# An accumulating DMA takes over half of GpSimd's adds, and ScalarE works thirteen banks ahead instead of seven

## The reference, cut to what matters

```python
e = stack([tbl_f[ids[:, f]] for f in range(39)], axis=1)      # 512 x 39 x 16
prev = e
for k in range(3):
    z = einsum('bmd,bhd->bdmh', e, prev).reshape(b, D, m * h)
    t = einsum('bdc,co->bdo', z, w[k]) + bias[k]
    t = transpose(t, (0, 2, 1)) / sqrt(sum(t * t))             # one norm for each example
    logit.append(t); prev = t
z = sum(concatenate(logit, axis=1), axis=-1)                   # 512 x 384
y = relu(relu([z, dense] @ W1 + b1) @ W2 + b2) @ W3
```

## Time and profile before

| | |
|---|---|
| median of 3 runs | 1070.53 us (1068.94 to 1072.45) |
| profiled execution | 1069.49 us, its span 1067.8 us |
| PE matmul / weight load busy | 97% / 74% of the span |
| DVE / ACT / POOL busy | 91% / 75% / 81% |
| granted TensorE clock | 0.998 of full speed |
| from job 12 to job 116 | 62.4 us for an iteration, eight jobs, nearly the same each time |

### The profile page before, as it was taken

The page is one execution under the profiler, slowest core; times in us unless marked ns, Lnnn a source line. Parts: engine busy times, 40 slices in busy tenths (PEclk is TensorE's granted clock), DMA queues, the critical chain, the costliest instruction groups (busy, mean ns, idle before and its releaser), DMA issues.

```text
span 1067.8 us, 18078 instructions
## 1 busy us (share of the span) xinstructions
PE 1036.7 (97%) x4384; PEld 788.9 (74%) x4384; DVE 971.2 (91%) x3328; ACT 796.2 (75%) x2671; POOL 864.0 (81%) x729
## 2 busy tenths in 40 slices
PE   2999999999999999999999999999999999999998
PEld 0466777878777787877778787777778777788883
DVE  2589999999999999999999999999999999999993
ACT  3476877868778787877778787787878778788872
POOL 6777888988888898888889898888988888576770
PEclk9999999999999999999999999999999999999999
DMA  6630030301403030120303012030300203000000
GB/s 189 158 95 12 3 83 3 84 2 17 126 4 83 3 84 2 22 65 3 83 3 84 1 21 66 3 83 3 84 2 11 75 3 83 1 1 1 1 1 1
DMA packets 59381, 44.02 MB, mean 41 GB/s; under 512 B 39177, under 2 KB 42121, under 8 KB 59146
## 3 DMA queue, kind: packets, MB, share of 16 engines
q1 hardware_dynamic: 51975, 36.49, 13.8%
q10 hardware_dynamic: 2179, 5.07, 1.4%
q0 software_dynamic: 5120, 1.29, 1.3%
HBM read 40.89 MB, written 1.94 MB: 40 GB/s over the span
## 4 chain that ended last, share of the span: by engine, by line
PE 67%; POOL 18%; DVE 6%; issue 5%; ACT 3%; DMA 1%; SPq 0%; POOLq 0%; DVEq 0%; ACTq 0%
POOL sums L415 13%; PE bank_a L705 10%; PE bank_d L705 9%; PE bank_d L707 9%; PE bank_d L706 9%; PE bank_a L707 9%; PE bank_a L706 9%; PE acc L775 8%; POOL gathered L398 4%; DVE sums L939 3%; ACT scaled L539 1%; ACT sums L539 1%; PE turned L748 1%; DVE prev L1004 1%; PE bank_d L876 1%
## 5 line engine op out<-in xcount | busy, mean ns | idle before, releaser
L415 POOL TENSOR_TENSOR sums<-sums,scaled 128x512 f32<-128x512 f32 (+1 forms) x512 | 646.5, 1264 | 140.4 <-ACT scaled L539 103.3
L939 DVE SCALAR_TENSOR_TENSOR sums<-bank_d,x_col,sums 128x128 f32<-128x128 f32 x2304 | 653.4, 337 | 47.1 <-PE bank_d L707 37.0
L539 ACT ACTIVATE scaled<-bank_a,x_col 128x128 f32<-128x128 f32 x1920 | 549.0, 383 | 129.5 <-PE bank_a L707 124.1
L705 PE MATMUL bank_d<-w_hi,prev_lo 128*128 128x512 f32 x640 | 283.9, 444 | 1.5 <-DVE sums L958 1.2
L705 PE MATMUL bank_a<-w_hi,prev_lo 128*128 128x512 f32 (+1 forms) x640 | 268.4, 419 | 3.5 <-ACT scaled L539 0.9
L707 PE MATMUL bank_d<-w_hi,prev_hi 128*128 128x512 f32 x640 | 252.5, 395 | 0.0
L706 PE MATMUL bank_d<-w_lo,prev_hi 128*128 128x512 f32 x640 | 252.2, 394 | 0.0
L707 PE MATMUL bank_a<-w_hi,prev_hi 128*128 128x512 f32 (+1 forms) x640 | 245.3, 383 | 0.0
L706 PE MATMUL bank_a<-w_lo,prev_hi 128*128 128x512 f32 (+1 forms) x640 | 244.9, 383 | 0.0
L539 ACT ACTIVATE sums<-bank_a,x_col 128x128 f32<-128x128 f32 x512 | 146.2, 371 | 75.3 <-PE bank_a L707 75.3
L398 POOL DMA_INDIRECT gathered<-in_table,idx x160 | 174.3, 1089 | 28.5 <-issue 17.9
(11 more groups left out here) (87 smaller groups left out, 537.2 us busy)
## 6 DMA issues: line engine op xcount, KB each, us to landing
x_pairs<-x_scratch SPq DMA_DIRECT2D x135, 156.0 KB
x_pairs<-x_scratch SPq DMA_DIRECT2D x96, 78.0 KB
gathered<-in_table,idx POOLq DMA_INDIRECT x160
x_pairs<-x_scratch SPq DMA_DIRECT2D x92, 22.0 KB
x_scratch<-gathered SPq DMA_DIRECT2D x16, 72.0 KB, 2.2
w_raw<-in_w ACTq DMA_DIRECT2D x1, 1024.0 KB, 5.0
w_raw<-in_w ACTq DMA_DIRECT2D x1, 896.0 KB, 10.1
w_raw<-in_w SPq DMA_DIRECT2D x1, 832.0 KB, 6.8
```

What stands on the lines that cost most here:

```text
L415: nc.gpsimd.tensor_tensor(out=sums[:, n % SUMS, 0:w, :], in0=sums[:, n % SUMS, 0:w, :], in1=scaled[:, a - 1, 0:w, :], op=ALU.add).then_inc ...
L539: op = nc.scalar.activation(to[:, i, :], bank_a[at % A_RING][:, i * UNITS:(i + 1) * UNITS], ACT.Copy, scale=x_of(c, q, a * PER_BANK + i))
L705: nc.tensor.matmul(to, lo, w_h, start=True, stop=False)
L939: nc.vector.scalar_tensor_tensor(out=taken(n, u) if u in LEFT else total, in0=taken(n, u), scalar=x_of(c, q, A_FIELDS + u), in1=total, op0 ...
```

## The change

In jobs 11 to 116 (`is_far`) GpSimd no longer adds four banks. Behind bank 4 it issues one DMA from `scaled` to `scaled` with an add on the way, which adds banks 3 and 4 to banks 1 and 2 (7 fields, 3584 bytes in each of 128 partitions, 448 KB), and then adds banks 1 and 2 to `sums`. These two adds stand five and six A banks behind bank 4 in GpSimd's list: first comes the DMA of the next job, then bank 1 of this job, then bank 2. `scaled` has two sets of buffers for it, for even and odd jobs; the second lies where raw weights lay. ScalarE writes banks 1 and 2 when the adds of the job two before are done, banks 3 and 4 when the DMA of that job is.

The lead grows from 7 to 13 banks over jobs 5 to 10 (six A banks in each of these jobs), and shrinks again over jobs 117 to 122 (four in each). With 13 the three-field bank is made in slot 1, bank 1 in slot 3, bank 2 in slot 4.

The gathers move from behind slots 1 and 2 to behind slots 3 and 4. `high` and `low` move: for layer 1 from behind slot 0 of step 5 to behind slot 3 of step 4, which is where `finish` of layer 1 stands; for layer 2 from behind slot 1 of step 6 to behind slot 0 of step 7. The norm of layer 0 moves on PE from behind place 1 of step 4 to behind place 9 of step 3, and on VectorE its sums and reciprocal come a few fields earlier.

```diff
-LEAD = 7
+LEAD, FAR_LEAD = 7, 13
...
+FAR_FROM, FAR_TO = 11, NJ - 12
+LEADS = [min(max(LEAD, LEAD + n - 5), FAR_LEAD, max(LEAD, FAR_LEAD + FAR_TO - n)) for n in range(NJ + 1)]
+FAR_ADDS = {1: A_BANKS, 2: A_BANKS + 1}
...
+ADDS_BEHIND = {at: [] for at in range(A_BANKS * NJ)}
+for _n in range(NJ):
+    for _a in range(1, A_BANKS):
+        if not is_far(_n):
+            ADDS_BEHIND[A_BANKS * _n + _a].append((_n, _a))
+        elif _a in FAR_ADDS:
+            ADDS_BEHIND[A_BANKS * _n + A_BANKS - 1 + FAR_ADDS[_a]].append((_n, _a))
...
-        FINISHES.append((0, _it + 1, (step_at(_it, 3), 0), (step_at(_it, 3), 14)))
+        FINISHES.append((0, _it + 1, (step_at(_it, 3), 0), (step_at(_it, 3), 8)))
...
-        NORMS.append(([(0, _it + 1)], (step_at(_it, 4), 1), (step_at(_it, 4), 0), (step_at(_it, 4), 6)))
+        NORMS.append(([(0, _it + 1)], (step_at(_it, 3), 9), (step_at(_it, 4), 0), (step_at(_it, 4), 4)))
...
-                HALVES_AT[_k + 1, _c] = (step_at(_c - 1, 5), 0) if _k == 0 else \
-                    (step_at(_c, 6), 1) if _c < CHUNKS - 1 else (step_at(_c, 5), 3)
+                HALVES_AT[_k + 1, _c] = (step_at(_c - 1, 4), 3) if _k == 0 else \
+                    (step_at(_c, 7), 0) if _c < CHUNKS - 1 else (step_at(_c, 5), 3)
...
-            def add_bank(at):
+            def add_banks(at):
+
+                if at >= A_BANKS * NJ:
+                    return
                 n, a = divmod(at, A_BANKS)
-                if n >= NJ or a == 0:
-                    return
-                pool.wait_ge(a_scaled, at + 1)
-                if a > 1:
-                    pool.wait_ge(a_added, ADDS * n + a - 1)
-                w = a_fields_of(a)
-                nc.gpsimd.tensor_tensor(out=sums[:, n % SUMS, 0:w, :], in0=sums[:, n % SUMS, 0:w, :],
-                                        in1=scaled[:, a - 1, 0:w, :], op=ALU.add).then_inc(a_added, 1)
+                if is_far(n) and a == A_BANKS - 1:
+                    pool.wait_ge(a_scaled, at + 1)
+                    nc.gpsimd.dma_start(pair_of(n, 1), pair_of(n, 3), accum_op=ALU.add).then_inc(pair_added[n % 2], 16)
+                for n, a in ADDS_BEHIND[at]:
+                    if is_far(n):
+                        pool.wait_ge(pair_added[n % 2], pairs_added_by(n))
+                    else:
+                        pool.wait_ge(a_scaled, at + 1)
+                    if a > 1:
+                        pool.wait_ge(a_added, ADDED[n, a - 1])
+                    w = PER_BANK if is_far(n) else a_fields_of(a)
+                    nc.gpsimd.tensor_tensor(out=sums[:, n % SUMS, 0:w, :], in0=sums[:, n % SUMS, 0:w, :],
+                                            in1=scaled_of(n, a)[:, 0:w, :], op=ALU.add).then_inc(a_added, 1)
...
+                begin = 1 if n < FAR_FROM else 3
+                for a in range(max(a_count(n), A_BANKS)):
+                    if a < a_count(n):
+                        add_banks(a_first(n) + a)
+                    if begin <= a < begin + per_step and first + a - begin < GATHERS:
+                        gather(it + 2, first + a - begin)
...
-                    if n >= 1:
-                        act.wait_ge(a_added, ADDS * (n - 1) + a)
-                    to = scaled[:, a - 1, :, :]
+
+                    was = n - 1 if n < FAR_FROM else n - 2
+                    if n == FAR_FROM:
+
+                        act.wait_ge(w_lo_made[1], len(W_PIECES[1]))
+                        act.wait_ge(w_lo_made[2], len(W_PIECES[2]))
+                    elif is_far(was) and a > max(FAR_ADDS):
+                        act.wait_ge(pair_added[was % 2], pairs_added_by(was))
+                    elif was >= 0:
+                        act.wait_ge(a_added, ADDED[was, a] if (was, a) in ADDED else added_all(was))
+                    to = scaled_of(n, a)
```

More of the change, by code:

```diff
@@ L67, with is_far, a_first, a_count @@
 JOB_AT = {j: n for n, j in enumerate(JOBS)}
+FAR_FROM, FAR_TO = 11, NJ - 12
+LEADS = [min(max(LEAD, LEAD + n - 5), FAR_LEAD, max(LEAD, FAR_LEAD + FAR_TO - n)) for n in range(NJ + 1)]
+FAR_ADDS = {1: A_BANKS, 2: A_BANKS + 1}
+def is_far(n):
+    return FAR_FROM <= n <= FAR_TO
+def a_first(n):
+    return A_BANKS * n + LEADS[n]
+def a_count(n):
+    return a_first(n + 1) - a_first(n) if n + 1 < NJ else A_BANKS
+ADDS_BEHIND = {at: [] for at in range(A_BANKS * NJ)}
[5 more added lines that the diff above has]
+            ADDS_BEHIND[A_BANKS * _n + A_BANKS - 1 + FAR_ADDS[_a]].append((_n, _a))
+ADDED = {}
+for _at in range(A_BANKS * NJ):
+    for _add in ADDS_BEHIND[_at]:
+        ADDED[_add] = len(ADDED) + 1
+def added_all(n):
+    return ADDED[n, max(FAR_ADDS) if is_far(n) else A_BANKS - 1]
 def step_at(it, q):
@@ L196, in cin_kernel @@
         identity = sb("identity", [128, 128])
-        w_raw = {k: sb(f"w{k}_raw", [128, FIELDS, UNITS]) for k in (1, 2)}
+        used = 28
+        with ExitStack() as first_life:
+            w_raw = {k: first_life.enter_context(nc.sbuf_tensor(f"w{k}_raw", [128, FIELDS, UNITS], f32)) for k in (1, 2)}
+        scaled_odd = []
+        for k in (1, 2):
+            sb(f"raw_rows{k}", [128, used, UNITS])
+            scaled_odd.append(sb(f"scaled_odd{k}", [128, 2, PER_BANK, UNITS]))
+            sb(f"raw_rest{k}", [128, FIELDS - used - 2 * PER_BANK, UNITS])
         w_hi = {k: sb(f"w{k}_hi", [128, FIELDS, UNITS], f32r) for k in (1, 2)}
@@ L281, in cin_kernel @@
         a_added = sem("a_added")
+        pair_added = [sem(f"pair_added{parity}") for parity in range(2)]
         d_ready = sem("d_ready")
@@ L319, in cin_kernel, with scaled_of, pair_of, pairs_added_by @@
         TOP_LOADS = 2 * 3 + 2
+        def scaled_of(n, a):
+            if n < FAR_FROM or n % 2 == 0:
+                return scaled[:, a - 1, :, :]
+            return scaled_odd[(a - 1) // 2][:, (a - 1) % 2, :, :]
+        def pair_of(n, a):
+            first = scaled[:, a - 1:a + 1, :, :] if n % 2 == 0 else scaled_odd[(a - 1) // 2][:, :, :, :]
+            return first.rearrange("p a i u -> p (a i u)")[:, 0:(PER_BANK + a_fields_of(A_BANKS - 1)) * UNITS]
+        def pairs_added_by(n):
+            return 16 * ((n - FAR_FROM) // 2 + 1)
         def a_fields_of(a):
@@ L447, in _ @@
                 gather(2, j)
-            for at in range(LEAD):
-                add_bank(at)
+            for at in range(LEADS[0]):
+                add_banks(at)
             for n in range(NJ):
@@ L459, in _ @@
                     start_chunk(it + 2)
-                for a in range(A_BANKS):
-                    add_bank(A_BANKS * n + LEAD + a)
-                    if 1 <= a <= per_step and first + a - 1 < GATHERS:
-                        gather(it + 2, first + a - 1)
+                begin = 1 if n < FAR_FROM else 3
[4 more added lines that the diff above has]
+                        gather(it + 2, first + a - begin)
                     for item, at in HALVES_AT.items():
@@ L652, in _ @@
                                  ACT.Copy).then_inc(prev_hi_made[1], 1)
[L653 removed]
+            for at in range(LEADS[0]):
                 scale_bank(at)
[L655 removed]
+                if at == LEADS[0] - 2:
                     square_x(1)
             for n in range(NJ):
[L658 to L659 removed]
+                for a in range(max(a_count(n), A_BANKS)):
+                    if a < a_count(n):
+                        scale_bank(a_first(n) + a)
                     if (n, a) in W2_HIGH_AT:
@@ L837, in _ @@
                     else:
-                        bank_for_act(A_BANKS * n + LEAD + a)
-                        a += 1
+                        until = a + 1 if place < len(PATTERN) - 1 else a_count(n)
+                        while a < until:
+                            bank_for_act(a_first(n) + a)
+                            a += 1
                     if place == 5 and n:
```

7 lines of the change are left out of this document (1 added, 6 removed).

## The result

The median of four runs is 1122.4 us (1116.4 to 1123.65), beside 1069.74 us for four runs of the kernel before: a ratio of 1.0479, interval 1.0447 to 1.0512. The kernel became slower, by 53 us where the forecast said 23, and lies outside its range of 1082 to 1104. The profiled execution spans 1121.9 us instead of 1067.8.

What follows compares the result with a forecast made beforehand. PE was taken as the bound. Losses of 31.2 us (13 x 1.11 + 14 x 1.0 + 13 x 0.1 + 1.5) less 8.2 gained gave +23.0, so 1093 us; forecast 1082 to 1104, wider range 1068 to 1138.

Steps and rivals of the forecast that it cites:

- the ring: PE's A banks, ring of two: ScalarE must end bank b about 0.16 us before bank b + 2's nominal start.
- the meeting: Step 7: VectorE's first `make_pairs` and GpSimd's add get in each other's way by some 0.8 us.
- the ramps: Jobs 5 to 10 and 117 to 122: same work, but job 8's `finish` and `high` cost some 1.5 us.
- steps 4 and 5: `finish` and `high` together behind slot 3 make slot 4 late: PE loses 1.11 us, less 0.21 gained in step 5.
- steps 7 and 0: `high` and `low` behind slot 0 delay issue and add: 0.68 us lost, 1.48 if the add is hit, 1.0 taken.
- The issue, t: GpSimd's time to issue the accumulating DMA: 0.98 us with the gap behind it, between bounds of 0.38 and 2.87.
- the issue costs twice a gather: Rival: issue of 1.92 us on GpSimd gives 1151 us, 1.4 gives 1117; chance of a dear issue 0.16.
- GpSimd starts 0.08 behind ...; issue 0.98, add 1.29: Light job, three-field bank's end to first add's end; slot 3 starts at 6.13 us, leaving 0.13 us in hand.
- the landing: The DMA's transfer, awaited 7.9 us after issue, takes 6.8 us at most, so it costs zero.
- the issue is cheap: Rival: an issue of 0.5 us on GpSimd gives 1075 us, 0.38 gives 1073; chance 0.16.
- The transfer lands late: Rival: the DMA lands beyond 7.9 us because SP's loads fill the engines, 1110 to 1150 us; chance 0.06.
- Faster: Rival: the lead absorbs step 4's late slot 4, leaving a gain of 0.63 us an iteration, 1062 us; chance 0.12.

Runs made afterwards that it cites:

- the version with one field: The changed kernel with the accumulating DMA cut to one field of seven, the other six fields' sums left out: 1115.77 us, 1.0439.
- adds first with one field: The changed kernel with each job's two adds ahead of the next job's DMA and the DMA cut to one field of seven: 1081.84 us, 1.0135.
- the lead alone: The changed kernel with all four adds on GpSimd and no DMA, keeping lead 13, both buffer sets, new places and gathers: 1076.85 us, 1.0054.
- adds first: The changed kernel with each job's two adds two A banks earlier, ahead of the next job's DMA and step 7's `low`: 1145.85 us, 1.0701.

## Why the prediction was partly right

The direction held, and so did the ring and most of the places where PE would wait. What failed is the sum for the path from ScalarE's three-field bank through GpSimd to the first add's end, which was too short where no `low` stands ahead of the issue, the start of each job's sum, and the terms for the meeting, the loads and the ramps; together the forecast was 31 us too small. The terms, against the profiled executions:

| | predicted | measured |
|---|---|---|
| steps 4 and 5, an iteration | +1.11 - 0.21 = 0.90 | 0.15 + 1.34 = 1.49 |
| steps 7 and 0 | +1.0 | 0.30 + 1.62 = 1.92 |
| step 3 | +0.1 | 0.17 |
| step 6 | -0.42 | -0.39 |
| steps 1 and 2 | 0 | -0.13 |
| 13 iterations | 21.5 | 39.8 |
| ramps | 1.5 | 5.7 |
| loads and landing (job 28) | 0 | 5.4 |
| start of the first job | 0 | 3.0, not of the change |

- **PE bounds, not GpSimd: right.** Half of GpSimd's adds taken away gave nothing by itself (the version without DMA, with two adds, is at 1083; the one with all four adds and the same lead is at 1077).
- **The ring of two, "PE needs the end of bank b 0.16 us before the nominal start of bank b + 2": right.** With the slot ends measured after the change the rule gives 0.35 lost in job 67 (measured 0.29), and for job 68 place 1, from slot 3's end at 619.46 + 7.38 + 1.14 = 627.98 against 626.66 + 0.70 - 0.16 = 627.20, 0.78 (measured 0.77).
- **"The issue, t ... I take 0.98": right**, 0.91 to 0.93 in the mean, 0.84 to 0.99 one by one; the add overlaps its end and is longer for it. The rival "the issue costs twice a gather" is out. The Trainium skill, "Collectives: The Full Stack", The bandwidth ceiling, speaks of two read descriptors for a reduce; no double price is seen on GpSimd, whatever the DMA engines do.
- **"GpSimd starts 0.08 behind ...; issue 0.98, add 1.29": the first step that failed.** The three add up to 2.35 us and measured 2.61 to 2.74, in all steps but 7: the issue starts 0.30 to 0.57 us behind the bank, and the add behind it takes 1.56 to 1.68. In job 66 slot 3 starts at 6.61 instead of 6.13, so the 0.13 in hand was gone; 0.35 short at slot 4 of a light job is what step 7 shows.
- **Each job summed from a light job's start: the second.** For steps 4 and 7 the forecast took ScalarE's times from job 59, where it is not behind. After the change it comes in late from the job before: slot 1 of step 4 ends at 4.20 instead of 3.68, and `high` of step 7 starts at 3.12 instead of 2.61. Of the 1.48 us that an iteration took beyond the forecast, 0.84 - 0.3 is the next point's; the 0.9 that is left, 0.59 of it in steps 4 and 5, goes with these two. Some 12 us of the 31. Runs: the version with one field keeps all of it, adds first with one field removes it, with 7.6, 7.0, 7.9, 6.9 and 6.9 in steps 3 to 7.
- **"If the add is hit, 1.48 is lost; I take 1.0": mis-sized.** The meeting of `make_pairs` and an add came every time, and on the second add, which delays slot 4. The 0.3 that the forecast had for it measured 0.84; moving `make_pairs` away gave 11 us of step 0. The Trainium skill, "SBUF — State Buffer", Who interferes with whom, has such a pair lock each other out; 2.09 us instead of 1.29 here agrees, and its sum would have been 7 us nearer.
- **"I cost it at zero", the landing: right in the change** (GpSimd never waits for it), **wrong beside it.** Its bound, "6.8 at most", did not hold either: behind the issues of step 7 in jobs 19 to 107 the last packet lands after 6.3 to 9.0 us, and only the late place of the adds covers this. `x_pairs` of job 28 come behind 1.3 MB of other loads: 5.4 us in the trace, 7 by the run that moved those loads. "The first of them is needed in step 7 and is hidden" held in every iteration but this one.
- **"The `finish` and `high` of job 8 ... cost some 1.5": mis-sized.** The ramp costs 6.0 to 6.5 on the way up and gives 0.85 back (2.8 with the adds all on GpSimd). Six more banks in jobs 5 to 10 are 6 x 0.70 = 4.2 us, and I took it as given that the jobs with four return all of them. The two parts: going up costs 6.0 with the lead alone, so it is not the DMA's; coming down, job 116 takes 8.15 with the change, 7.53 without its DMA, and 6.2 with the lead alone or with adds first: there the late adds cost more than the issue. Why the lead alone returns only 2.8 of the 4.2 is not shown.
- **Of the signs:** step 6's idle time gone, POOL at 65%, step 5's place 3 late by 1.3, all as said; light jobs at 6.91 (step 7 takes 7.20), slot 3 of a light job 0.4 late (6.61 against 5.72, 0.9) and 64 us an iteration were not.

**Still open.** Why an issue starts 0.30 to 0.57 us behind its semaphore where an add takes 0.08, and why it is 0.30 in step 3 and 0.54 in step 6 though GpSimd stood idle for over 2 us before both: the runs show that it is so, not what GpSimd does in it. How much the late start and the longer add each cost is told from the trace alone; no run tests the two apart. Nor does one settle why the lead alone makes job 28 late: it has the later gathers too.

The rivals: "the issue costs twice a gather" and "the issue is cheap" fell with its 0.91 to 0.93. "The transfer lands late" is not what happens in the change, but it is what happens (1146 us) as soon as its adds stand earlier. "Faster" needed step 4 to lose under 0.6; it lost more, and the adds and the ring carried it to PE.
